# A two-layer graph convolution on one core: edge counts by windows of 12 destinations instead of 16, and another order of the row fetches

## What is computed

```
def _sage_sum(h, src, dst, Ws, Wn, b):
    h_neigh = jax.ops.segment_sum(h[src], dst, num_segments=1250)
    return h @ Ws + h_neigh @ Wn + b
h = jnp.maximum(_layernorm(x, axis=-1), 0.0)
h = _sage_sum(h, src, dst, Ws1, Wn1, b1)
h = _sage_sum(h, src, dst, Ws2, Wn2, b2)
out = x + h
```

## Time and profile before

| | |
|---|---|
| median of 3 runs | 656.73 us (655.3 to 657.68) |
| the profiled execution | 655.63 us, of it the span of instructions 653.8 us |
| PE busy | 640.9 us, 98% of the span |
| VectorE, ScalarE, GpSimd busy | 286.0, 174.3, 210.3 us |
| granted TensorE clock | full from the first slices on |
| count matmuls (L1101) | 400, from 68.7 to 155 us |

### The profile page before, as it was taken

How to read it: one execution, slowest core, us unless ns; L and a number is a source line. 1 busy time by engine, 2 the same in 40 slices (tenths; PEclk the granted TensorE clock), 3 DMA queues, 4 the chain that set the end, 5 groups by cost and what they waited for, 6 DMA issues and landing times.

```text
span 653.8 us, 8550 instructions
## 1 busy us (share of the span) xinstructions
PE 640.9 (98%) x3304; PEld 556.3 (85%) x3304; DVE 286.0 (44%) x392; ACT 174.3 (27%) x292; POOL 210.3 (32%) x198
## 2 busy tenths in 40 slices
PE   7999989999999999999999999999999999999997
PEld 5788778887899989999999988888888888887885
DVE  6763898871112111210022483325387987611111
ACT  5454243222123222313233122211334333100000
POOL 6224352000256666576580158003214012000000
PEclk9999999999999999999999999999999999999999
DMA  8622321003165676466754686444322242011111
GB/s 299 213 53 43 94 90 49 33 34 128 57 216 201 209 237 246 143 227 239 257 224 163 230 259 218 154 145 155 126 82 81 72 157 95 32 65 49 61 48 63
DMA packets 62726, 90.63 MB, mean 139 GB/s; under 512 B 16546, under 2 KB 34988, under 8 KB 62679
## 3 DMA queue, kind: packets, MB, share of 16 engines
q1 hardware_dynamic: 42342, 76.08, 34.6%
q10 hardware_dynamic: 20336, 13.91, 6.8%
HBM read 58.49 MB, written 31.48 MB: 138 GB/s over the span
## 4 chain that ended last, share of the span: by engine, by line
PE 62%; DMA 1%; DVE 0%; issue 0%; ACT 0%; POOL 0%; SPq 0%; DVEq 0%
PE PS L1274 29%; PE PS L1290 14%; PE PS L1237 10%; PE PS L1245 9%; DMA quarters<-ws_in 1%; DVE W_st L1021 0%; POOL prep_sum L624 0%; ACT W_st L750 0%; DVE s L1089 0%; ACT prep L801 0%; SPq L493 0%; DVEq L1088 0%
## 5 line engine op out<-in xcount | busy, mean ns | idle before, releaser
L1274 PE MATMUL PS<-right,left 128*128 128x512 f32 x840 | 190.6, 389 | 0.0
L1274 PEld LDWEIGHTS PS<-right,left 128*128 128x128 f32 x840 | 157.7, 188 | 32.7
L1109 PE MATMUL PS<-W,HT 128*128 128x512 f32 (+1 forms) x456 | 114.7, 399 | 2.7 <-ACT y_out L674 1.8
L1237 PE MATMUL PS<-HT,W_st 128*128 128x416 f32 (+1 forms) x576 | 110.7, 352 | 2.4 <-DVE W_st L1021 1.4
L1237 PEld LDWEIGHTS PS<-HT,W_st 128*128 128x128 f32 x576 | 107.9, 188 | 4.4 <-issue 3.4
L1109 PEld LDWEIGHTS PS<-W,HT 128*128 128x128 f32 (+1 forms) x456 | 81.3, 185 | 21.3 <-ACT y_out L674 2.9
L1245 PE MATMUL PS<-AT,y_st 128*128 128x416 f32 (+2 forms) x480 | 92.2, 351 | 0.0
L1245 PEld LDWEIGHTS PS<-AT,y_st 128*128 128x128 f32 (+1 forms) x480 | 90.1, 188 | 0.8
L657 POOL TENSOR_TENSOR left_sum<-h1T 128x640 f32<-128x640 f32 x24 | 41.9, 1747 | 150.2 <-PE PS L1274 119.9
L624 POOL TENSOR_TENSOR prep_sum<-quarters 128x512 f32<-128x512 f32 x40 | 52.7, 1320 | 100.0 <-PE PS L1109 62.8
L1290 PE MATMUL PS<-y_high,AT 128*128 128x512 f32 (+1 forms) x200 | 78.3, 392 | 0.0
(11 more groups left out here) (96 smaller groups left out, 476.9 us busy)
## 6 DMA issues: line engine op xcount, KB each, us to landing
sums_dram<-prep SPq DMA_DIRECT2D x40, 512.0 KB, 2.9
right<-sums_dram SPq DMA_DIRECT2D x40, 512.0 KB, 3.5
y_dram<-y_out ACTq DMA_DIRECT2D x18, 256.0 KB, 2.0
y_st_raw<-y_dram ACTq DMA_DIRECT2D x8, 576.0 KB
s<-x_in SPq DMA_DIRECT2D x18, 256.0 KB
out<-s SPq DMA_DIRECT2D x18, 256.0 KB
xin<-x_in SPq DMA_DIRECT2D x8, 512.0 KB, 11.6
W_raw<-wn_in SPq DMA_DIRECT2D x16, 256.0 KB, 5.1
```

The lines of the kernel that those rows point to most:

```text
L1109: ins = nc.tensor.matmul(PS[:r, bank, :], HT[:, a, k, t * P:t * P + r], W[:, k, b, :], start=first and m == 0, stop=last and m == 2)
L1237: ins = nc.tensor.matmul(PS[:, banks[c], 0:w_], W_st[:, a, k, :], HT[:, b, k, o_:o_ + w_], start=k == 0 and m == 0, stop=False)
L1274: ins = nc.tensor.matmul(PS[:, BANKS2[g % 8], :], left[:, k, a, i * P:(i + 1) * P], right[:, KB - 1 - k, b, :], start=k == 0 and j == 0, s ...
```

## The change

Windows have 12 destinations, rows have 4 edges, and 106 windows replace 80, so a window takes four count matmuls of 120 columns, a group has 4 windows (27 groups as before), and there are 5 one-hot buffers. A window's 128 rows hold 512 edges; with these inputs no window needs more than 482. The first edge of every sixth row is sampled, so every 24th. The edge list is read as 122 full partitions of 336 edges and one of 258, whose rest VectorE fills beforehand with 2047 (a new memset, for which SyncE waits before the edge DMAs, four of them now). A row fetch has ten windows instead of eight: 11 fetches. Fetches 0 to 6 stand before the list as before, then come all eight slabs, and fetches 7 to 10 stand behind slab 7. `src_parts` and `samples` share their place, so the sampling waits for all three casts. The diff, cut:

```diff
-WIN = 16
-NW = NPAD // WIN
-WPT = P // WIN
-ROW = 5
+WIN = 12
+NW = 2 * -(-N // (2 * WIN))
+FETCH = 10
+NFETCH = -(-NW // FETCH)
+ROW = 4
 ROWX = 16
-EROWS = E // ROW
-SAMPLE = 3
-EP = 125
-EPP = E // EP
-RPP = EPP // ROW
+SAMPLE = 6
+EP = 123
+RPP = 84
+EPP = RPP * ROW
+TAIL = E - (EP - 1) * EPP
+EROWS = EP * RPP
+NOWHERE = 2047
-GROUP = 3
+GROUP = 4
-HOT = 4
+HOT = 5
-SPW = WPT // 2
+SPF = FETCH // 2
+def fetched(a):
+
+    return range(a * FETCH, min((a + 1) * FETCH, NW))
@@ sync_order
-    yield ("windows", EARLY - 1)
     for p, event in enumerate(stage1_order()):
         if event[:2] == ("y1", NT - 1):
             yield ("slab", event[2])
-            if event[2] == 2:
-                yield ("windows", EARLY)
         if event == ("y1", 2 * NT - 1, 6):
             yield ("w_st", 0)
         if p in ends and ends[p] == NT - 1:
-            yield ("windows", EARLY + 1)
+            yield from (("windows", a) for a in range(EARLY - 1, NFETCH))
@@ sync
-            sp.dma_start(edge_ints[:, 0, :], src.rearrange("(p e) -> p e", p=EP)).then_inc(edges_in, 16)
-            sp.dma_start(edge_ints[:, 1, :], dst.rearrange("(p e) -> p e", p=EP)).then_inc(edges_in, 16)
+            sp.wait_ge(edges_padded, 1)
+            for part, ends in enumerate((src, dst)):
+                sp.dma_start(edge_ints[0:EP - 1, part, :],
+                             ends[0:(EP - 1) * EPP].rearrange("(p e) -> p e", p=EP - 1)).then_inc(edges_in, 16)
+                sp.dma_start(edge_ints[EP - 1:EP, part, 0:TAIL],
+                             ends[(EP - 1) * EPP:E].rearrange("(p e) -> p e", p=1)).then_inc(edges_in, 16)
@@ gpsimd
-            for a in range(NT):
-                pool.wait_ge(windows_in[a], WPT * 16)
+            for a in range(NFETCH):
+                pool.wait_ge(windows_in[a], len(fetched(a)) * 16)
@@ vector
-                dve.wait_ge(edges_cast, 1)
+                dve.wait_ge(edges_cast, 3)
+            nc.vector.memset(edge_ints[96:EP, :, TAIL:EPP], NOWHERE).then_inc(edges_padded, 1)
-                dve.wait_ge(rebased, u // SPW + 1)
+                dve.wait_ge(rebased, u // SPF + 1)
```

More of the change, by code:

```diff
@@ L279, in gnn_kernel @@
         edge_ints = at("edge_ints", [EP, 2, EPP], I32, o); o += up(2 * EPP * 4)
-        src_parts = at("src_parts", [EP, 2, EPP], I32, o); o += up(2 * EPP * 4)
-        samples = at("samples", [EP, NSAMP, NW], F16, o); o += up(NSAMP * NW * 2)
+        src_parts = at("src_parts", [EP, 2, EPP], I32, o)
+        samples = at("samples", [EP, NSAMP, NW], F16, o); o += up(max(NSAMP * NW * 2, 2 * EPP * 4))
         pad_row = at("pad_row", [P, ROWX], F16, o); o += up(ROWX * 2)
@@ L337, in gnn_kernel @@
         PSF = PS[:, :, :].rearrange("p b n -> p (b n)")
-        edges_in = sem("edges_in"); consts_in = sem("consts_in"); b2_in = sem("b2_in")
+        edges_padded = sem("edges_padded"); edges_in = sem("edges_in"); consts_in = sem("consts_in"); b2_in = sem("b2_in")
         x_in_t = [sem(f"x_in_{t}") for t in range(NT)]; x_in_first = sem("x_in_first")
@@ L346, in gnn_kernel @@
         sampled = sem("sampled"); counted = sem("counted"); row_found = sem("row_found")
-        windows_in = [sem(f"windows_in_{a}") for a in range(NT)]
+        windows_in = [sem(f"windows_in_{a}") for a in range(NFETCH)]
         clipped = sem("clipped"); rebased = sem("rebased")
@@ L441, in load_windows @@
                 _, rows = nc.values_load_multi_w_load_instructions(
-                    row_i[0:1, a * WPT:(a + 1) * WPT], engines=(mybir.EngineType.SP,), min_val=0, max_val=EROWS,
-                    skip_runtime_bounds_check_because="a count of sampled edges times 3, less 3 and at least 0: at most EROWS - 3")
-                for j in range(WPT):
-                    sp.dma_start(window_edges[:, a * WPT + j, :],
-                                 edge_rows[bass.ds(rows[j], P), :]).then_inc(windows_in[a], 16)
+                    row_i[0:1, fetched(a)[0]:fetched(a)[-1] + 1], engines=(mybir.EngineType.SP,), min_val=0, max_val=EROWS,
+                    skip_runtime_bounds_check_because="a count of sampled edges times 6, less 6 and at least 0: at most EROWS - 6")
+                for w, row in zip(fetched(a), rows):
+                    sp.dma_start(window_edges[:, w, :], edge_rows[bass.ds(row, P), :]).then_inc(windows_in[a], 16)
             sp.wait_ge(rows_saved, 32)
@@ L595, in _ @@
                                    allow_small_or_imprecise_dtypes=True).then_inc(iotas, 1)
-            for a in range(NT):
-                pool.wait_ge(windows_in[a], WPT * 16)
-                rows = window_edges[:, a * WPT:(a + 1) * WPT, :]
+            for a in range(NFETCH):
+                pool.wait_ge(windows_in[a], len(fetched(a)) * 16)
+                these = slice(fetched(a)[0], fetched(a)[-1] + 1)
+                rows = window_edges[:, these, :]
                 place = rows[:, :, 2 * ROW:3 * ROW]
@@ L606, in pairs @@
                 def pairs(tile):
-                    return tile[:, a * SPW:(a + 1) * SPW, :, :].rearrange("p u i e -> p u e i")
+                    return tile[:, these.start // 2:these.stop // 2, :, :].rearrange("p u i e -> p u e i")
                 nc.gpsimd.tensor_copy(pairs(pair_m), in_pairs(0))
-                nc.gpsimd.tensor_tensor(place, place, win_start[:, a * WPT:(a + 1) * WPT].unsqueeze(2).to_broadcast([P, WPT, ROW]),
+                nc.gpsimd.tensor_tensor(place, place, win_start[:, these].unsqueeze(2).to_broadcast([P, len(fetched(a)), ROW]),
                                         ALU.subtract).then_inc(clipped, 1)
@@ L910, in cast_edges @@
             def cast_edges():
-                dve.wait_ge(edges_in, 32)
+                dve.wait_ge(edges_in, 64)
                 nc.vector.tensor_scalar(src_parts[:, 0, :], edge_ints[:, 0, :], P - 1, None, ALU.bitwise_and).then_inc(src_split, 1)
```

2 lines of the change are left out of this document (1 added, 1 removed).

## The result

The changed kernel takes 664.19 us (median of 6 runs, 660.22 to 667.47), beside 656.01 us for the kernel before (6 runs, 654.39 to 659.24): a ratio of 1.0132, 95% interval 1.0104 to 1.0161. It is 1.3% slower. The prediction had said 654.8 us, within 651.8 to 657.8, and so it was wrong in sign and in size. The profiled execution of the changed kernel took 666.24 us, its span is 664.4 us where the one before has 653.8.

What follows compares the result with a forecast made beforehand. TensorE, busy 98% of the span, was taken as the bound: 1.7 us late by group 8, then 3.3 won over 18 shorter beats and 0.3 in the last group, -1.9 us in all: 654.8 us, range 651.8 to 657.8.

Steps and rivals of the forecast that it cites:

- The matmul's price: Count matmuls on TensorE: 55 ns apart at 120 columns instead of 72 at 160, bounds 54 and 72.
- Rival 3: Slower by PE: count matmuls stay 72 ns apart despite fewer columns, beat 3.27 us, +3.0 us, 659.7; chance 0.05.
- rival 5: Row keys through GpSimd come late for VectorE's late pairs: -1.9 + 1 to 3 us; chance 0.10.
- my 5.0: TensorE's gain in us if nothing waited: 26 beats each 0.183 shorter, plus 0.26 from the last group.
- The step from slab 0 to the end: Slab 0's issue on SyncE sets VectorE's start, hence PE's end; each us there is a us at the end.
- Two more edge DMAs cost SyncE 0.8 us before the x tiles: SyncE's front: the added edge DMAs cost 0.8 us of queue time, counted as nothing in the total.
- come 10 us later: Readers of the x tiles start 10 us later, so delay from the added edge DMAs was costed at nothing.
- if it is gone, some tenths are added to slab 0: Larger edge_rows write, 323 KB for 258, covered by the sampled counts' wait; without cover, some tenths of a us.
- is 0.53, with the gap behind it 0.55: SyncE's register load of row numbers per fetch, in us; used to put slab 0 2.55 us later.
- Rival 2: Slower by SyncE: fetches or edge rows cost more; turning point slab 0 at 77.35, at 79.5 +2.1 us; chance 0.13.
- the 3.1 us: Irregular extra time within the 40.23 us of 64 row fetches ahead of slab 0, kept whole in the forecast.
- two waits of 0.6 us that were forecast, for pairs 11 and 15: PE idling twice 0.6 us for VectorE's one-hot pairs, after waits of about 3 and 1.3 us.

Runs made afterwards that it cites:

- fetch_of_8: The changed kernel with 8 windows in a row fetch instead of 10, so 56 instead of 70 ahead of slab 0; 649.62 us, ratio 0.9873.
- edges_wide: tails_first plus edge loads split into 112 + 10 partitions and the edge_rows write into 112 + 11; 660.31 us, ratio 1.0079.
- fetch_of_12: The changed kernel with row fetches of 12 windows, six of them (72 windows) ahead of slab 0; 659.74 us, ratio 1.0072.
- loads_of_eight: The changed kernel, fetches of ten kept, with the first 70 rows read by register loads of 8 x 8 and 6 values; 660.16 us, ratio 1.0066.
- tails_first: The changed kernel with the two one-partition edge loads issued before Wn1's loads; 667.19 us, ratio 1.0134.
- loads_of_five: The changed kernel with each fetch's ten row numbers read by two register loads of five; 667.02 us, ratio 1.0162.
- wide_of_8: edges_wide with 8 windows in a row fetch instead of 10; 647.49 us, ratio 0.9876.
- before_edges_narrow: The kernel before with edge DMAs split into 122 + 3 partitions and the edge_rows write into 123 + 2, in place of 125; 659.59 us, ratio 1.0048.
- before_loads_of_ten: The kernel before with its first 64 rows read by six register loads of ten and one of four, not eight of eight; 660.24 us, ratio 1.0067.

## Why the prediction was wrong

**What held.** The matmul's price: sixteen take 1.04 us with 215 ns for one, (1.04 - 0.215) / 15 = 55 ns apart, as forecast, and the beat is 3.017 us over groups 5 to 26 (3.015). hot_m and hot_n take 0.60 and 0.57 us, a pair 1.17 (1.19), a subtraction 0.60 (0.61). Rival 3 is out, and with it the 81 ns of the Trainium skill's TensorE: Matmul & The Clock Gate (Back-to-back issue gap). GpSimd's keys (rival 5) cost nothing: VectorE waited 0.5 us for them once, and PE not at all. From group 0 to group 26 the undisturbed gain is 4.72 us, against 26 x 0.183 = 4.76; the 0.26 of the last group, which makes up my 5.0, does not show.

The step from slab 0 to the end held too, and that is what the prediction hung on. It had group 26 at 152.6 for slab 0 at 75.45, and a us for a us, so group 26 at slab 0 + 77.15:

| kernel | slab 0 issued | group 26 by the step | group 26 measured |
|---|---|---|---|
| fetch_of_8 | 72.45 | 149.6 | 149.59 |
| edges_wide | 81.40 | 158.6 | 159.22 |
| fetch_of_12 | 81.66 | 158.8 | 159.38 |
| loads_of_eight | 81.99 | 159.1 | 160.53 |
| tails_first | 85.40 | 162.6 | 163.36 |
| changed kernel | 87.56 | 164.7 | 166.18 |
| loads_of_five | 88.66 | 165.8 | 166.87 |
| wide_of_8 | 67.42 | 144.6 | 146.69 |

In the last row PE's own beats are what counts: 68.26 + 26 x 3.01 = 146.5. The row of fetch_of_8 is exact. The six others are 0.6 to 1.5 us over the line, and these are the kernels in which the clock fell to 0.5 in the stall.

**What failed** was the size of slab 0's delay, by three terms:

1. "Two more edge DMAs cost SyncE 0.8 us before the x tiles". The edge loads as changed cost 5.4 us more than before: x tiles from 14.11 instead of 8.67. I had priced the added DMAs by the issue time of their neighbours and not asked what the changed partition count of the old ones does. That the readers "come 10 us later" did not cover it either: group 0 came 1.3 us late by the edges' own late landing. The stall behind it swallowed that here; in before_edges_narrow it makes nearly all of the loss.
2. The write of edge_rows: "if it is gone, some tenths are added to slab 0". The cover in the profile before was thin: the write landed at 30.98 and the register load began at 31.8. It was issued 5.3 us later and landed at 36.70. Terms 1 and 2 together put the first register load from 31.81 to 36.72, 4.9 us; that load took 1.58 us for 0.73, another 0.85; and 0.14 earlier had been forecast. That is the 5.9.
3. The register load "is 0.53, with the gap behind it 0.55" was measured on eight values and taken for ten. For the six loads between the fetches it was 6.2 us short. I had named bounds for the matmul, whose size changed, and none for the load, whose size changed too.

Rival 2 (slower, by SyncE) was the right one, with its place and its turning point (slab 0 at 77.35). Its price stopped at 79.5, since I thought only of more irregular time on top of the 3.1 us. "Against: it needs 1.9 us of new extras" was wrong: two known quantities had changed size. A fourth term was missing altogether: a long stall costs more than its length, as PE comes out of it at the lower clock. I put the 166.18 - 164.7 = 1.5 us by which the changed kernel is over the line down to it. From start to start, the nine products behind group 3 took 3.94 us in place of 2.15, and the counts of group 4 1.38 in place of 0.86, 2.3 us more; two waits of 0.6 us that were forecast, for pairs 11 and 15, did not come. That leaves 1.1 of the 1.5 us; the rest is open, and no run has the stall without the lower clock.

The sum, in the profiled executions: group 26 was forecast 1.6 us earlier than before and came 12.0 later. Of the 13.6 us between, 5.9 are the edge front, 6.2 the loads, and the 1.5 left over are what I put down to the clock.

## What to carry to other kernels

When a change alters a size (partitions of a transfer, values in a load), every instruction that has this size needs its price looked at anew, on the queue as well as on the engine that the change is for: here 5 us won on TensorE cost 12 us on SyncE. Give DMAs a partition count with a large divisor up to 16, splitting 123 into 112 + 11 if need be, as edges_wide does; and read row numbers in registers by multiples of four from a multiple of four. And find the one issue time on which the end hangs: a us there was a us at the end, within 1.5 us, in seven kernels of the table, so a bound for it is a bound for the time.

## What the runs showed of the hardware that I had not expected

- A DMA's issue can hold its queue long after others went through in 0.35 us: 1.66 and 3.46 us for a one-partition load behind 122-partition ones, 0.34 and 0.23 for the same loads ahead of Wn1; 8.91 us for 4 KB of pad rows in the kernel before, 10.27 in the changed one, 6.82 in edges_wide. That a full ring of the few engines used is what holds it is my reading of it; the runs show only that the time follows the partition counts of the transfers ahead.
- A register load of n values costs 0.28 us for one, 0.31 for an aligned four, 0.53 for eight, 0.75 for twelve, and 0.2 us for each value left over behind the fours, or for every value of a load that starts elsewhere: 0.94 for ten from a multiple of four, 2.07 for ten from elsewhere. (Aligned means that the load starts at a multiple of four.) Runtime: NRT & Kernel Launch, in the Trainium skill (Instruction fetch mechanics), gives about 200 ns a register for TENSOR_LOAD "even for bulk", where it speaks of the runtime's own loads from device memory; the single values here agree, the aligned fours, at 0.22 us for each further four, do not.
- The granted clock fell to 0.5 in PE's long stalls and stayed there for some us after PE had work again: to 100.4 us in the changed kernel, where the work began at 92.83 after 13.65 us; to 87.8 in before_loads_of_ten, where it began at 83.11 after 4.47. Around the wait of 1.86 us in before_edges_narrow, before 88.36, it stayed at 1.0.
- The stretch from the first feature product to the second layer's first, which no edit touches, took 198.9 to 201.9 us in most traces, but 205.1 in tails_first and 209.9 in fetch_of_8. In these two PE waited 2.2 to 4.9 us for h1T or W_st once or twice, and the clock fell to 0.5 at each (at 253.9 us, and at 238.2 and 292.8). So a single profiled execution is good to a few us at its end, and the comparisons above go by group 26.
